# Eight gate rows, a block table and a tail: four batches' gates stored ahead, the dispatch reordered, the last two blocks in one branch

## The chip, the cores and the metric

The kernel runs on one core of a Trainium2 chip. The metric is the device time of one execution in microseconds. The core has five engines that run at once and meet at semaphores: TensorE (PE: matmuls and transposes into PSUM banks), VectorE (DVE), ScalarE (ACT), GpSimd (POOL) and SyncE (SP, which here only issues DMAs). PEld is the weight load of TensorE, which overlaps its matmuls.

## The reference, cut to what matters

```
u = stack([mean, max, std]) of each batch and channel, of the normalised x      # 8 batches, 512 channels
g = sigmoid(BN(sum((u - median(u)) ** 3 * cfc_w)))                              # one gate per batch and channel
x = x + ln_c(x) * g
t = tokens(x)                                                                   # 2048 tokens of 512
xn = ln_t(t)
e = argmax(xn @ router_w.T); w = sigmoid(max logit)                             # one of 8 experts
out = t + w * glu_e(xn) + glu_shared(xn)     # glu(x) = (silu(x @ wg) * (x @ wu)) @ wd, all 512x512
```

## The kernel before, in words

The host only lays the arrays out, tokens by channels. There are 16 tiles of 128 tokens (two to a batch) and, behind them, blocks of 128 tokens that are sorted by expert. Each engine has its own program, written out by hand in the order in which it runs; nothing is scheduled, so the order of the code is the order of the engine, and an instruction waits for the semaphores named ahead of it.

Stage 1 measures batches and channels. Stage 2 finds the median of each batch by a search of seven steps. On TensorE `keep_warm` puts matmuls into it whose results nobody reads. At its end ScalarE turns `z` into `gates` with Sigmoid and then loads the table of Silu with the small `warm` activation (L571). Meanwhile GpSimd makes the low parts of weight set 0 (L397), and `w_raw` holds the raw weights of a set, one third each for GATE, UP and DOWN.

Stage 3 takes the 16 tiles. For a tile, ScalarE normalises it (`norm_a`), VectorE multiplies it by the batch's gates and adds (`gate_tile`, L760 to L773), and normalises it again (`norm_tile`). The gates of a batch must be spread over all 128 tokens: `spread_gate(b)` on TensorE transposes four broadcast columns of `gates` into the bank `mb`, and `gate_tile` reads the bank. There is one such bank, so a batch's gates are spread only when the tiles of the batch before have used theirs (`gate_used`); `GATES_AFTER` says after which iteration n this happens. The tile is transposed (`prepare`, bank `tx`), split into a high and a low part (`x_hi` on ScalarE, `x_lo` on VectorE), multiplied by the shared expert's gate and up matrices (`gate_product`, `up_product`, bank `GU`, 12 matmuls each), gated (`silu_gate`, `gated`), transposed again (`transpose_h`, bank `th`), split again (`h_hi`, `h_lo`), multiplied by the down matrix (`down_product`, bank `yb`) and added (`add_shared`). `route` makes the router's logits, in `th` too.

Stage 4, the dispatch, runs among the last five tiles of the shared expert. `choose` picks the experts, `rank` on TensorE counts, for each token, the tokens ahead of it with the same expert, and, in 16 matmuls of their own (`COUNTS`, L1205), each expert's tokens. On VectorE `slots_of_tokens`, `place` and `fields` make matrices from that, `fill_slots` on TensorE (L1213) multiplies them, and `slot_tables`, `block_experts` and `block_table` make the indices and a table of blocks.

Stage 5 runs the blocks, 20 of them with these inputs. `groups` loops over 24 places. In the first 12 places `step` runs without a question; in the others each engine compares `needed` with the place. `step(b)` makes the gate and up products of block b + 1, transposes the hidden tile of block b and the input of block b + 2, and makes the down product of block b. `last(b)` has only the transpose and the down product. GpSimd gathers inputs (`gather_x`, `gather_z`) and scatters results (`scatter`).

The time of matmuls and transposes is best read from the start of one group to the start of the next.

Of the kernel before, what the change touches and what calls it, by code (L numbers as in the profile page):

```python
# [34 lines left out]
SPLIT_AFTER = (4, 5, 7)  # L35
GATES_AFTER = {0: 2, 2: 3, 3: 4, 5: 5, 6: 6, 8: 7}
# [7 lines left out]
def program(nc, B, x_tok, conv_par, router, weights, xn_d, z_d, out):  # L44
# [12 lines left out]
    with ExitStack() as ctx:  # L57
# [63 lines left out]
        slotinfo = sb("slotinfo", [P, 3, NB])  # L121
# [49 lines left out]
        z_ready = sem("z_ready")  # L171
        g_ready = sem("g_ready")
# [49 lines left out]

        def tally(i):

            return (yb, mb)[i % 2][:, i:i + 1]
# [43 lines left out]
        def groups(eng, step, last):  # L269


            needed = needed_blocks(eng)
            with eng.Fori(0, SURE // RING) as j:
                for u in range(RING):
                    step(j * RING + u, u, j, 0)
            with eng.Fori(0, (NB - SURE) // RING) as j:
                for u in range(RING):
                    b = j * RING + (SURE + u)
                    with eng.If(needed > b + 1):
                        step(b, u, j, SURE // RING)  # L280
                    with eng.If(needed == b + 1):
                        last(b, u, j, SURE // RING)
# [3 lines left out]
        def _(sp):  # L286
# [11 lines left out]
            for k in range(3):  # L298
                sp.wait_ge(wlo, k + 1)
                load_w(1, k)  # L300
# [26 lines left out]
        def _(pool):  # L327
# [124 lines left out]
            for b in range(NB):  # L452
# [25 lines left out]
        def _(act):  # L478
# [91 lines left out]
            act.activation(gates[:, :, :], z[:, :, :], ACT.Sigmoid, scale=-1.0).then_inc(g_ready, 1)  # L570
            act.activation(warm[:, 1:2], eps[:, 0:1], ACT.Silu).then_inc(warmed, 1)  # L571
# [45 lines left out]
            def last(b, u, j, base):  # L617
                h_hi(b + NT, u % 2)

            act.wait_ge(tables, 1)  # L620
            next_set(table_entries(act, 0, range(DUE_GU_COL, FIRST_COL + 1)))
            groups(act, step, last)
# [3 lines left out]
        def _(dve):  # L626
# [133 lines left out]
            def gate_tile(t, u, batch):  # L760
# [3 lines left out]
                dve.wait_ge(gates_spread, batch + 1)  # L764
                dve.tensor_tensor(buf, buf, mb[:, :], ALU.mult).then_inc(gate_used, 1)
# [159 lines left out]
            def slot_tables():  # L925
# [3 lines left out]
                tok, row, wgt = (slotinfo[:, i, :] for i in range(3))  # L929
# [54 lines left out]
            def add_routed(n, b, u, count):  # L984
                dve.wait_ge(y_done, n + 1)
                dve.wait_ge(zg_in[u], count)
                dve.scalar_tensor_tensor(out=zg[:, u, :], in0=yb[:, :], scalar=slotinfo[:, 2, ds(b, 1)], in1=zg[:, u, :],  # L987
                                         op0=ALU.mult, op1=ALU.add).then_inc(y_used, 1)
# [50 lines left out]
            groups(dve, step, last)  # L1039
# [3 lines left out]
        def _(pe):  # L1043
            pe.wait_ge(consts, N_CONSTS)

            def keep_warm(n):

                for _ in range(n):
                    pe.matmul(th[:, :], ones_bf[:, :], ones_bf[:, 0:1].to_broadcast([P, C]), start=True, stop=True)  # L1049
# [50 lines left out]
            def spread_gate(b):  # L1100

                if b == 0:
                    pe.wait_ge(g_ready, 1)
                else:
                    pe.wait_ge(gate_used, 2 * b)
                for k in range(KC):
                    last = pe.transpose(mb[:, k * P:(k + 1) * P], gates[:, b, k:k + 1].to_broadcast([P, P]), ident[:, :])  # L1107
# [16 lines left out]
            def product(dst, left, q, k):  # L1124

                i = 0
                for kc in range(KC):
                    for lp, wp in ((HI, HI), (HI, LO), (LO, HI)):
                        last = pe.matmul(dst, left[:, lp, kc, :], wset(q, k, wp, kc), start=(i == 0), stop=(i == 3 * KC - 1))  # L1129
                        i += 1  # L1130
                return last
# [11 lines left out]
            def down_product(n, parity, q, before):  # L1143
# [3 lines left out]
                product(yb[:, :], hT[:, parity], q, DOWN).then_inc(y_done, 1)  # L1147

            def route(t, slot):

                pe.wait_ge(xlo, t + 1)
                if not (isinstance(t, int) and t == 0):
# [13 lines left out]
            keep_warm(8)  # L1166
            spread_gate(1)
            keep_warm(2)
# [26 lines left out]
            def rank():  # L1195
# [61 lines left out]
            def last(b, u, j, base):  # L1257
# [5 lines left out]
            groups(pe, step, last)  # L1263
# [36 lines left out]
```

## Time and profile before

| what | value |
|---|---|
| median of 3 runs | 431.53 us (430.38 to 432.97) |
| the profiled execution | 430.49 us |
| its span, first to last instruction | 428.7 us |
| TensorE's mean granted clock in it | 0.965 of full speed |
| busy: PE, DVE, ACT, POOL | 384.1, 259.6, 158.2, 135.8 us |

Busy time is the sum of an engine's instructions. The profiled execution is 1.04 us below the median, and 1.8 us of it lie outside the span.

### The profile page before, as it was taken

To read this page: it belongs to the slowest core of one execution; us is meant where nothing else is said; L and a number is where in the kernel's file an instruction comes from. 1 tells how busy PE (TensorE), PEld (TensorE's weight loads), DVE (VectorE), ACT (ScalarE), POOL (GpSimd) and SP (SyncE) were. 2 spreads that over 40 slices of the span, in tenths; PEclk is the share of its full clock that TensorE was granted. 3 is DMA by queue.
4 is the path that set the end of the run, shared out by engine and by line. 5 is a ranking of instruction groups with operands and counts; after the bars stand their busy time and mean duration, and the time that the engine had idled before them with its cause. 6 is when DMAs were issued, how large, how long until landed. Compare 5 with 4: busy or idle time off the path is not lost.

```text
span 428.7 us, 6732 instructions
## 1 busy us (share of the span) xinstructions
PE 384.1 (90%) x1942; PEld 313.2 (73%) x1943; DVE 259.6 (61%) x494; ACT 158.2 (37%) x262; POOL 135.8 (32%) x188
## 2 busy tenths in 40 slices
PE   1455576999999999999989999999999999999993
PEld 1343134888888888888878888888888888888882
DVE  5995868455575795754686557636556653776322
ACT  4787861212223423221112335434144624354110
POOL 5676832000010010003112034633426442446201
PEclk9757988999999999999999999999999999999998
DMA  8900341011121342311004086765636764742300
GB/s 275 407 7 2 124 170 49 26 49 50 49 75 50 130 145 93 126 72 50 26 25 122 26 317 201 253 232 203 216 86 249 271 256 144 253 173 91 94 24 29
DMA packets 15865, 56.18 MB, mean 131 GB/s; under 512 B 2591, under 2 KB 2591, under 8 KB 12384
## 3 DMA queue, kind: packets, MB, share of 16 engines
q1 hardware_dynamic: 10960, 40.93, 26.8%
q0 software_dynamic: 4880, 14.95, 9.6%
q8 instruction: 13, 0.21, 0.2%
q14 instruction: 12, 0.10, 0.1%
HBM read 43.28 MB, written 13.63 MB: 133 GB/s over the span
## 4 chain that ended last, share of the span: by engine, by line
PE 80%; DVE 10%; issue 3%; ACT 3%; POOL 2%; DMA 1%; DVEq 0%; POOLq 0%; ACTq 0%
PE GU L1129 45%; PE yb L1129 22%; PE tx L1114 4%; PE th L1121 3%; PE th L1156 3%; DVE search_junk L709 1%; DVE bn_parts L664 1%; ACT tiles L492 1%; POOL tok_rstd L375 1%; DMA x_sb<-x_tok 1%; PE mb L1107 1%; PE th L1049 1%; DVE scratch L922 1%; ACT scratch L503 1%; DVE bn_parts L669 1%
## 5 line engine op out<-in xcount | busy, mean ns | idle before, releaser
L1129 PE MATMUL GU<-w_parts,xT 128*128 (+1 forms) x864 | 214.6, 398 | 0.0
L1129 PEld LDWEIGHTS GU<-w_parts,xT 128*128 128x128 f32 x864 | 159.4, 189 | 31.8
L1129 PE MATMUL yb<-w_parts,hT 128*128 (+1 forms) x432 | 105.4, 393 | 1.9 <-DVE hT L791 1.9
L563 ACT ACTIVATE hT<-th 128x512 fp32r<-128x512 f32 x36 | 21.5, 598 | 195.1 <-PE th L1121 195.1
L1129 PEld LDWEIGHTS yb<-w_parts,hT 128*128 128x128 f32 x432 | 80.1, 188 | 18.2 <-issue 2.1
L430 POOL DMA_INDIRECT out<-x_sb,scatidx x20 | 37.3, 1864 | 93.7 <-DVE x_sb L987 93.7
L812 DVE TENSOR_TENSOR w_parts<-w_raw,w_parts 128x2048 f32 (+1 forms) x24 | 54.9, 2288 | 6.7 <-issue 6.4
L797 DVE TENSOR_TENSOR hidden<-hidden,GU 128x512 f32<-128x512 f32 x36 | 24.8, 688 | 42.9 <-PE GU L1129 42.8
L480 ACT ACTIVATE w_parts<-w_raw 128x2048 f32 (+1 forms) x24 | 45.2, 1910 | 3.8 <-issue 3.7
L404 POOL TENSOR_TENSOR x_rstd<-x_mv,eps 128x1 f32<-128x1 f32 x16 | 3.2, 203 | 120.5 <-DVE x_mv L773 120.5
L791 DVE TENSOR_TENSOR hT<-th,hT 128x512 fp32r<-128x512 f32 x36 | 24.8, 688 | 23.1 <-ACT hT L563 23.0
L553 ACT ACTIVATE xT<-tx 128x512 fp32r<-128x512 f32 x37 | 22.0, 596 | 41.1 <-PE tx L1114 41.1
L987 DVE SCALAR_TENSOR_TENSOR x_sb<-yb,slotinfo,x_sb 128x512 f32<-128x512 f32 x20 | 15.0, 749 | 31.9 <-PE yb L1129 29.2
L1061 PE MATMUL GU<-ident,tiles 128*128 128x128 f32 x64 | 14.6, 406 | 21.3 <-ACT tiles L492 21.3
L1061 PEld LDWEIGHTS GU<-ident,tiles 128*128 128x128 f32 x64 | 12.0, 214 | 23.3 <-issue 16.0
L421 POOL DMA_INDIRECT tiles<-xn_d,tokidx x21 | 20.2, 961 | 24.3 <-DVE slotinfo L939 18.2
L425 POOL DMA_INDIRECT x_sb<-z_d,tokidx x20 | 19.4, 971 | 25.9 <-DMA z_d<-x_sb 20.1
L782 DVE TENSOR_TENSOR xT<-tx,xT 128x512 fp32r<-128x512 f32 x37 | 25.3, 683 | 3.5 <-ACT xT L553 3.4
L1114 PE MATMUL tx<-ident,tiles 128*128 128x128 f32 x148 | 22.7, 277 | 2.7 <-DVE xT L782 1.5
L802 DVE TENSOR_TENSOR x_sb<-x_sb,yb 128x512 f32<-128x512 f32 x16 | 11.0, 686 | 19.5 <-PE yb L1129 19.4
L558 ACT ACTIVATE hidden<-GU 128x512 f32<-128x512 f32 x36 | 21.7, 602 | 3.0 <-PE GU L1129 3.0
L1114 PEld LDWEIGHTS tx<-ident,tiles 128*128 128x128 f32 x148 | 17.9, 142 | 5.3 <-DVE tiles L778 3.4
(194 smaller groups left out, 352.2 us busy)
## 6 DMA issues: line engine op xcount, KB each, us to landing
w_raw<-weights SPq DMA_DIRECT2D x27, 1024.0 KB, 5.2
x_sb<-x_tok SPq DMA_DIRECT2D x8, 512.0 KB, 8.0
xn_d<-tiles SPq DMA_DIRECT2D x16, 256.0 KB, 2.0
z_d<-x_sb SPq DMA_DIRECT2D x16, 256.0 KB, 2.0
tiles<-xn_d,tokidx POOLq DMA_INDIRECT x21, 4.5
x_sb<-z_d,tokidx POOLq DMA_INDIRECT x20, 5.5
out<-x_sb,scatidx POOLq DMA_INDIRECT x20, 6.9
conv<-conv_par SPq DMA_DIRECT2D x1, 10.0 KB, 10.7
```

The costliest lines, as they stand in the source:

```text
L430: pool.indirect_dma_start(out[:, :], rows(scatidx, b), zg[:, b % RING, :], None, bounds_check=T - 1, oob_is_err=False).then_inc(o_out[b % ...
L480: act.activation(hi, raw, ACT.Copy).then_inc(whi, 1)
L553: act.activation(xT[:, slot, HI, :, :], tx[:, :].rearrange("p (k t) -> p k t", k=KC), ACT.Copy).then_inc(xhi, 1)
L558: act.activation(hidden[:, parity, :], gu(parity, GATE), ACT.Silu).then_inc(silu, 1)
L563: act.activation(hT[:, parity, HI, :, :], th[:, :].rearrange("p (k t) -> p k t", k=KC), ACT.Copy).then_inc(hhi, 1)
L782: dve.tensor_tensor(xT[:, slot, LO, :, :], tx[:, :].rearrange("p (k t) -> p k t", k=KC), xT[:, slot, HI, :, :].bitcast(F32), ALU.subtract) ...
L791: dve.tensor_tensor(hT[:, parity, LO, :, :], th[:, :].rearrange("p (k t) -> p k t", k=KC), hT[:, parity, HI, :, :].bitcast(F32), ALU.subtr ...
L797: dve.tensor_tensor(hidden[:, parity, :], hidden[:, parity, :], gu(parity, UP), ALU.mult).then_inc(hid_ready, 1)
L812: dve.tensor_tensor(lo, w_raw[:, k, :, :], hi.bitcast(F32), ALU.subtract).then_inc(wlo, 1)
L1061: last = pe.transpose(aT[:, k, h * P:(h + 1) * P], tiles[:, t % RING, k * P:(k + 1) * P], ident[:, :])
L1114: last = pe.transpose(tx[:, k * P:(k + 1) * P], src[:, k * P:(k + 1) * P], ident[:, :])
L1129: last = pe.matmul(dst, left[:, lp, kc, :], wset(q, k, wp, kc), start=(i == 0), stop=(i == 3 * KC - 1))
```

## The change

There are four parts.

1. Gates. `spread_gate` of batches 2 to 5 moves ahead of the first tile. It goes into bank `th`, ScalarE copies each one into the DOWN third of `w_raw` (free once set 0 is split), and `gate_tile` reads it there. `gates_stored` passes between them. Batches 0, 1, 6 and 7 still use `mb`. SyncE loads the DOWN third of set 1 later, ahead of `store_z(6)`, when tile 11 has used its gates; ScalarE and VectorE split it one iteration later (`SPLIT_AFTER`).
2. Counts. The 16 matmuls of `COUNTS` go; the matmuls of the ranks are made one tile wider and one more is added.
3. Order on VectorE in the dispatch.
4. `last_two` in place of `last`: the last two blocks in one branch. The transpose of the last hidden tile stands in the middle of the down product ahead of it, the last down product goes into `mb`, and the input of a block behind the last is neither gathered nor transposed.

```
-SPLIT_AFTER = (4, 5, 7)
-GATES_AFTER = {0: 2, 2: 3, 3: 4, 5: 5, 6: 6, 8: 7}
+SPLIT_AFTER = (4, 5, 8)
+GATES_AFTER = {6: 6, 8: 7}
+STORED_GATES = range(2, 6)
...
+        def gate_rows(batch):
+
+            return w_raw[:, DOWN, batch - STORED_GATES.start, :] if batch in STORED_GATES else mb[:, :]
...
-                    with eng.If(needed > b + 1):
+                    with eng.If(needed > b + 2):
                         step(b, u, j, SURE // RING)
-                    with eng.If(needed == b + 1):
-                        last(b, u, j, SURE // RING)
+                    with eng.If(needed == b + 2):
+                        last_two(b, u, j, SURE // RING)
...
-            for k in range(3):
+            for k in (GATE, UP):
                 sp.wait_ge(wlo, k + 1)
                 load_w(1, k)
...
+                if STORED_GATES.stop * 2 - 1 in (PREPARED[n] if n < len(PREPARED) else ()):
+                    sp.wait_ge(wlo, 3)
+                    sp.wait_ge(gate_used, STORED_GATES.stop * 2)
+                    load_w(1, DOWN)
...
-                    with pool.If(needed > c):
+                    with pool.If(needed > c + 1):
                         fetch_x(c + 1)
...
             act.activation(gates[:, :, :], z[:, :, :], ACT.Sigmoid, scale=-1.0).then_inc(g_ready, 1)
+            act.wait_ge(wlo, 3)
+            for b in STORED_GATES:
+                act.wait_ge(gates_spread, b)
+                act.activation(gate_rows(b), th[:, :], ACT.Copy).then_inc(gates_stored, 1)
             act.activation(warm[:, 1:2], eps[:, 0:1], ACT.Silu).then_inc(warmed, 1)
...
-                dve.wait_ge(gates_spread, batch + 1)
-                dve.tensor_tensor(buf, buf, mb[:, :], ALU.mult).then_inc(gate_used, 1)
+                if batch in STORED_GATES:
+                    dve.wait_ge(gates_stored, batch - STORED_GATES.start + 1)
+                else:
+                    dve.wait_ge(gates_spread, batch + 1 if batch > 1 else 1 + batch * (len(STORED_GATES) + 1))
+                dve.tensor_tensor(buf, buf, gate_rows(batch), ALU.mult).then_inc(gate_used, 1)
...
             gated(n + 1, 0)
+            slots_of_tokens()
             add_shared(n)
-            slots_of_tokens()
+            place()
             h_lo(n + 1, 0)
-            place()
+            fields()
             gated(n + 2, 1)
-            fields()
             add_shared(n + 1)
...
-            def last(b, u, j, base):
+            def last_two(b, u, j, base):
                 h_lo(b + NT, u % 2)
+                gated(b + (NT + 1), 1 - u % 2)
+                h_lo(b + (NT + 1), 1 - u % 2)
                 add_routed(b + NT, b, u, j * 16 + 16 * (base + 1))
+                add_routed(b + (NT + 1), b + 1, (u + 1) % RING, j * 16 + 16 * (base + 1 + (u + 1) // RING), mb)
...
             spread_gate(0)
-            keep_warm(8)
+            for b in STORED_GATES:
+                spread_gate(b)
+                keep_warm(1, yb)
             spread_gate(1)
-            keep_warm(2)
+            keep_warm(2, yb)
...
-                for i in range(NT - 1):
-                    pe.matmul(mb[:, (i + 1) * E:NT * E].rearrange("p (t e) -> p t e", e=E), ones_bf[:, :],
-                              oh[:, i * E:(i + 1) * E].unsqueeze(1).to_broadcast([P, NT - 1 - i, E]),
-                              start=False, stop=(i == NT - 2))
+                pe.matmul(mb[:, COUNTS], ones_bf[:, :], oh[:, 0:E], start=False, stop=False)
                 for i in range(NT):
-                    last = pe.matmul(mb[:, COUNTS], ones_bf[:, :], oh[:, i * E:(i + 1) * E], start=(i == 0), stop=(i == NT - 1))
+                    after = NT - (i == 0) - i
+                    last = pe.matmul(mb[:, (i + 1) * E:(i + 1 + after) * E].rearrange("p (t e) -> p t e", e=E), ones_bf[:, :],
...
-            def last(b, u, j, base):
-                at, = table_entries(pe, b, range(SET_COL, SET_COL + 1))
-                transpose_h(b + NT, u % 2)
-                down_product(b + NT, u % 2, at % 2, at * 3)
+            def last_two(b, u, j, base):
+                n = b + NT
+                at, after = table_entries(pe, b, range(SET_COL, SET2_COL + 1))
+                gate_product(n + 1, 1 - u % 2, 1 - u % 2, after % 2, after * 3)
+                transpose_h(n, u % 2)
+                up_product(n + 1, 1 - u % 2, 1 - u % 2, after % 2, after * 3)
+                down_product(n, u % 2, at % 2, at * 3, lambda: transpose_h(n + 1, 1 - u % 2))
+                pe.wait_ge(wlo, after * 3 + 3)
+                pe.wait_ge(hlo, n + 2)
+                product(mb[:, :], hT[:, 1 - u % 2], after % 2, DOWN).then_inc(y_done, 1)
```

Three places show what the engines issue in which order. The first is TensorE at the passage from stage 2 to stage 3. Before:

```order
L1049 MATMUL th<-ones_bf 128x512 x9
L1107 MATMUL mb<-ident,gates 128x128 x4
L1049 MATMUL th<-ones_bf 128x512 x8
L1107 MATMUL mb<-ident,gates 128x128 x4
L1049 MATMUL th<-ones_bf 128x512 x2
L1114 MATMUL tx<-ident,tiles 128x128 x8
L1129 MATMUL GU<-w_parts,xT 128x512 x12
```

The same place of the changed kernel, from the second spread on (the first two rows stand there four times):

```order
L1134 MATMUL th<-ident,gates 128x128 x4
L1071 MATMUL yb<-ones_bf 128x512
...
L1134 MATMUL mb<-ident,gates 128x128 x4
L1071 MATMUL yb<-ones_bf 128x512 x2
L1141 MATMUL tx<-ident,tiles 128x128 x8
L1156 MATMUL GU<-w_parts,xT 128x512 x12
```

Eight matmuls of `keep_warm` became four spreads with one such matmul behind each, and each of these spreads but the first waits for ScalarE's copy of the one before it. The second place is VectorE in the dispatch, from the last instruction of `slots_of_tokens` to `add_shared(n + 1)`. Before:

```order
L900 CAST tiles<-tiles 128x32
L791 TENSOR_TENSOR hT<-th,hT 128x512
L904 TENSOR_TENSOR scratch<-iota_f,tiles 128x2048
L906 TENSOR_TENSOR tiles<-iota_f,tiles 128x384
L797 TENSOR_TENSOR hidden<-hidden,GU 128x512
...
L922 TENSOR_TENSOR scratch<-tiles 128x16x24 x6
L802 TENSOR_TENSOR x_sb<-x_sb,yb 128x512
```

After:

```order
L919 CAST tiles<-tiles 128x32
L821 TENSOR_TENSOR x_sb<-x_sb,yb 128x512
L923 TENSOR_TENSOR scratch<-iota_f,tiles 128x2048
L925 TENSOR_TENSOR tiles<-iota_f,tiles 128x384
L810 TENSOR_TENSOR hT<-th,hT 128x512
...
L941 TENSOR_TENSOR scratch<-tiles 128x16x24 x6
L816 TENSOR_TENSOR hidden<-hidden,GU 128x512
L821 TENSOR_TENSOR x_sb<-x_sb,yb 128x512
```

`slots_of_tokens` now stands ahead of the first addition of `yb`, `place` ahead of the split of `th`, and `fields` ahead of the product with `GU`. The third place is TensorE in the branch of the changed kernel for the last two blocks, around the middle of the first down product (the rows marked ISA set up a register):

```order
L1156 MATMUL yb<-w_parts,hT 128x512 x2
L1148 MATMUL th<-ident,hidden 128x128 x4
L1156 ISA
L1156 MATMUL yb<-w_parts,hT 128x512
...
L1156 MATMUL yb<-w_parts,hT 128x512 x2
L1297 REGISTER_ALU
L1156 ISA
L1156 MATMUL mb<-w_parts,hT 128x512
```

Before, the four transposes of `hidden` stood behind the whole down product, in a branch of their own.

## Rows read from the trace of the kernel before

**Rows 1.** Page, part 1: busy time, share of the span and instructions of each engine

```profile
PE 384.1 (90%) x1942; PEld 313.2 (73%) x1943; DVE 259.6 (61%) x494; ACT 158.2 (37%) x262; POOL 135.8 (32%) x188
```

**Rows 2.** Timeline of PE inside the loop of tiles: start us, us, engine, line

```profile
91.34 0.60 PE L1107 MATMUL mb<-ident,gates 128*128 128x128 f32 x4
91.69 1.04 PE L1156 MATMUL th<-router_parts,xT 128*128 128x16 f32 x8
```

**Rows 3.** Timeline of PE, end of stage 2 to the first products

```profile
63.90 2.12 PE L1049 MATMUL th<-ones_bf 128*128 128x512 bf16 x8
...
69.61 0.66 PE L1114 MATMUL tx<-ident,tiles 128*128 128x128 f32 x4 [1.16 <-DVE tiles L778]
71.78 1.08 PE L1114 MATMUL tx<-ident,tiles 128*128 128x128 f32 x4 [1.50 <-DVE xT L782]
72.51 3.96 PE L1129 MATMUL GU<-w_parts,xT 128*128 128x512 f32 x12
```

**Rows 4.** Timeline of ACT in the same stretch

```profile
62.41 1.28 ACT L571 ACT_TABLE_LOAD   x1
63.70 0.20 ACT L571 ACTIVATE warm<-eps 128x1 f32<-128x1 f32 x1
70.31 0.60 ACT L553 ACTIVATE xT<-tx 128x512 fp32r<-128x512 f32 x1 [6.41 <-PE tx L1114]
```

**Rows 5.** Windows of PE: stretch, its length, busy, granted clock, DMA share, GB/s

```profile
43.00:55.50 12.50, 6.67 (x33) 1.00 0.46 168
...
67.70:71.20 3.50, 1.42 (x9) 0.99 0.20 75
71.20:74.60 3.40, 2.82 (x9) 0.50 0.20 77
```

**Rows 6.** Timeline of PE in the dispatch

```profile
204.66 0.54 PE L1205 MATMUL mb<-tiles,ones_bf 128*128 128x8 bf16 x16
205.06 2.97 PE L1129 MATMUL yb<-w_parts,hT 128*128 128x512 f32 x12
...
216.50 2.88 PE L1129 MATMUL GU<-w_parts,xT 128*128 128x512 f32 x12
220.66 1.17 PE L1213 MATMUL mb<-scratch 128*128 128x144 bf16 x16 [1.27 <-DVE scratch L922]
```

**Rows 7.** Timeline of DVE in the dispatch

```profile
204.36 0.69 DVE L797 TENSOR_TENSOR hidden<-hidden,GU 128x512 f32<-128x512 f32 x1 [1.52 <-PE GU L1129]
...
208.68 0.28 DVE L888 TENSOR_TENSOR tiles<-tile_start,mb 128x128 f32<-128x128 f32 x1
...
211.96 0.69 DVE L791 TENSOR_TENSOR hT<-th,hT 128x512 fp32r<-128x512 f32 x1
...
215.35 0.69 DVE L797 TENSOR_TENSOR hidden<-hidden,GU 128x512 f32<-128x512 f32 x1
...
217.70 2.90 DVE L922 TENSOR_TENSOR scratch<-tiles 128x384 bf16<-128x384 bf16 x6
```

**Rows 8.** Timeline of PE over the last three blocks

```profile
406.32 2.88 PE L1129 MATMUL yb<-w_parts,hT 128*128 x12
409.05 2.89 PE L1129 MATMUL GU<-w_parts,xT 128*128 x12
411.77 0.60 PE L1121 MATMUL th<-ident,hidden 128*128 128x128 f32 x4
...
412.56 3.01 PE L1129 MATMUL GU<-w_parts,xT 128*128 x12
415.41 2.89 PE L1129 MATMUL yb<-w_parts,hT 128*128 x12
418.14 0.60 PE L1121 MATMUL th<-ident,hidden 128*128 128x128 f32 x4
420.62 3.03 PE L1129 MATMUL yb<-w_parts,hT 128*128 x12 [1.89 <-DVE hT L791]
```

**Rows 9.** Timeline of DVE, the last hidden tile

```profile
415.68 0.69 DVE L797 TENSOR_TENSOR hidden<-hidden,GU 128x512 f32<-128x512 f32 x1 [1.35 <-PE GU L1129]
```

More of the change, by code:

```diff
@@ L171, in program @@
         z_ready = sem("z_ready")
+        gates_stored = sem("gates_stored")
         g_ready = sem("g_ready")
@@ L267, in needed_blocks, with groups @@
             return table_entries(eng, 0, range(TOTAL_COL, TOTAL_COL + 1))[0]
-        def groups(eng, step, last):
+        def groups(eng, step, last_two):
             needed = needed_blocks(eng)
@@ L615, in step @@
                 next_set(table_entries(act, b + 1, range(DUE_GU_COL, FIRST_COL + 1)))
-            def last(b, u, j, base):
+            def last_two(b, u, j, base):
                 h_hi(b + NT, u % 2)
+                silu_gate(b + (NT + 1), 1 - u % 2)
+                h_hi(b + (NT + 1), 1 - u % 2)
             act.wait_ge(tables, 1)
             next_set(table_entries(act, 0, range(DUE_GU_COL, FIRST_COL + 1)))
-            groups(act, step, last)
+            groups(act, step, last_two)
         @block.vector
@@ L928, in slot_tables @@
                 S = mb[:, SLOTS].rearrange("p (f b) -> p f b", f=FIELDS)
-                tok, row, wgt = (slotinfo[:, i, :] for i in range(3))
+                tok, row, wgt = (slotinfo[:, i, 0:NB] for i in range(3))
                 own(dve.tensor_copy(tok, S[:, 0, :]))
@@ L982, in block_table, with add_routed @@
                 dve.engine_nop().then_inc(tables, 1)
-            def add_routed(n, b, u, count):
+            def add_routed(n, b, u, count, bank=yb):
                 dve.wait_ge(y_done, n + 1)
                 dve.wait_ge(zg_in[u], count)
-                dve.scalar_tensor_tensor(out=zg[:, u, :], in0=yb[:, :], scalar=slotinfo[:, 2, ds(b, 1)], in1=zg[:, u, :],
+                dve.scalar_tensor_tensor(out=zg[:, u, :], in0=bank[:, :], scalar=slotinfo[:, 2, ds(b, 1)], in1=zg[:, u, :],
                                          op0=ALU.mult, op1=ALU.add).then_inc(y_used, 1)
@@ L1038, in _ @@
                 lo_of(DOWN, at)
-            groups(dve, step, last)
+            groups(dve, step, last_two)
         @block.tensor
@@ L1044, in _, with keep_warm @@
             pe.wait_ge(consts, N_CONSTS)
-            def keep_warm(n):
+            def keep_warm(n, bank=th):
                 for _ in range(n):
-                    pe.matmul(th[:, :], ones_bf[:, :], ones_bf[:, 0:1].to_broadcast([P, C]), start=True, stop=True)
+                    pe.matmul(bank[:, :], ones_bf[:, :], ones_bf[:, 0:1].to_broadcast([P, C]), start=True, stop=True)
             for b in range(B):
@@ L1103, in spread_gate @@
                     pe.wait_ge(g_ready, 1)
+                elif b in STORED_GATES:
+                    pe.wait_ge(gates_stored, b - STORED_GATES.start)
+                elif b == STORED_GATES.stop:
+                    pe.wait_ge(gate_used, 4)
                 else:
                     pe.wait_ge(gate_used, 2 * b)
+                bank = th if b in STORED_GATES else mb
                 for k in range(KC):
-                    last = pe.transpose(mb[:, k * P:(k + 1) * P], gates[:, b, k:k + 1].to_broadcast([P, P]), ident[:, :])
+                    last = pe.transpose(bank[:, k * P:(k + 1) * P], gates[:, b, k:k + 1].to_broadcast([P, P]), ident[:, :])
                 last.then_inc(gates_spread, 1)
@@ L1122, in transpose_h, with product @@
                 last.then_inc(th_done, 1)
-            def product(dst, left, q, k):
+            def product(dst, left, q, k, amid=None):
                 i = 0
@@ L1130, in product @@
                         i += 1
+                    if kc == 1 and amid:
+                        amid()
                 return last
@@ L1141, in up_product, with down_product @@
                 product(gu(parity, UP), xT[:, slot], q, UP).then_inc(u_done, 1)
-            def down_product(n, parity, q, before):
+            def down_product(n, parity, q, before, amid=None):
                 pe.wait_ge(wlo, before + 3)
                 pe.wait_ge(hlo, n + 1)
-                product(yb[:, :], hT[:, parity], q, DOWN).then_inc(y_done, 1)
+                product(yb[:, :], hT[:, parity], q, DOWN, amid).then_inc(y_done, 1)
             def route(t, slot):
                 pe.wait_ge(xlo, t + 1)
-                if not (isinstance(t, int) and t == 0):
+                if t == 0:
+                    pe.wait_ge(gates_stored, len(STORED_GATES))
+                else:
                     pe.wait_ge(logits_used, t)
```

8 lines of the change are left out of this document (5 added, 3 removed).

## The prediction, as it was made before the changed kernel ran

> **What bounds the kernel now.** I read the page's busy times first, then the chain that ended last, then the timelines of TensorE and of the engine that releases it at the places which the diff touches. TensorE is busy 90% of the span [rows 1]; between the first product and the end nearly every group on it starts where the one before ends. So what is taken out of its queue there is gained whole. It waits in three places that this change touches: before the first product [rows 3], at `fill_slots` in the dispatch [rows 6], and before the last down product [rows 8]. The sum is made against the profiled execution, 430.49 us, which lies 1.04 us below the median of 431.53.
>
> **Gates in the loop.** A spread takes 0.35 us of TensorE's queue, 91.34 to 91.69 [rows 2]. Four of six leave the loop, each of them between groups that run back to back: 4 x 0.36 = 1.4 us less. The readers lose nothing: `gate_tile` multiplies from SBUF instead of a bank, for which I take no price (bounds: 0, or 0.1 us for each of 8 tiles on VectorE, which in this stage waits for TensorE). The copies' room is the DOWN third of `w_raw`. Its load for set 1 moves behind tile 11, in SyncE's queue ahead of `store_z(6)` and of all later stores; one issue there delays stores that nobody needs before the dispatch ends. The split of it moves from iteration 8 to 9 of 11; its user is the first routed down product, many products later. Both at nothing.
>
> **Gates before the first tile.** This is the part that costs. Four rounds of spread, copy, spread run one behind the other, since `th` is one bank. From the start of four transposes to the start of ScalarE's conversion it takes 0.70 us (69.61 to 70.31), an ACT conversion of 128x512 takes 0.60 [rows 3, 4], and a transpose that waited for VectorE started about 0.15 after it: 1.45 a round. The first begins where the keep-warm matmuls begin now, 63.90 [rows 3], and, at the lower clock, takes about 0.25 more. The last copy ends at 63.90 + 0.25 + 4 x 1.45 - 0.15 = 69.8. Behind it in ScalarE's queue stand the load of Silu's table, 1.28, and `warm`, some 0.1 before the next can start [rows 4], so `x_hi(0)` starts at 71.2, not at 70.31. `x_lo(0)` and the transposes of tile 1 follow it, so those start at about 72.67 instead of 71.78 [rows 3]: 0.9 us later. What was hidden between 62.4 and 70.3 (the table load) is no longer.
> What follows depends on the clock. Now it is at the lower level (1.2 GHz, 0.50 granted) from 71.2 to 74.6, after a stretch in which TensorE was busy 1.42 of 3.50 us; in the search it was busy 6.67 of 12.5 and stayed at 2.4 GHz [rows 5]. The first product takes 3.96 us there against 2.88 later [rows 3, 6]. In the new order TensorE has, between 64 and 70.5, five spreads, six keep-warm matmuls and the transposes of tile 0 at even distances, some 0.9 us of busy time in a round of 1.45 by the same count (0.60 for a spread, 0.27 for one matmul), more than in the search. I hold it likelier than not that it stays at 2.4 GHz. Then tile 1 takes 0.36, the product starts at 73.0 and the next group at 75.9, instead of 72.51 + 3.80 = 76.3: 0.45 gained in spite of the later start. If the lower level comes where it came before, half of the 0.9 is lost, 0.4; if it only moves along, all 0.9.
> A rule speaks against this part. The Trainium skill, "ScalarE: Activation LUTs", section What ACT_TABLE_LOAD costs, puts a switch of table at 1283 ns and a drain of 1380 ns more. The trace has 62.41 to 63.70, 1.29 us, with no drain before the next activation [rows 4]. With the page's figure as an estimate the first conversion would come 1.38 later still and the sum below would be smaller by that.
>
> **Counts with ranks.** The 16 matmuls of the counts take 204.66 to 205.06, 0.40 us, 25 ns each [rows 6]. Two are added, 0.05, and the others are 8 columns wider, about 0.03 in all: 0.32 less. Waits on them end earlier too.
>
> **Dispatch order.** `fill_slots` starts at 220.66; the product ahead of it starts at 216.50 and takes 2.72 to the next start when nothing waits [rows 6, 8]: 1.44 us of stall, which ends with the last of the field products of VectorE, 217.70 + 2.90 = 220.60 [rows 7]. Before, `add_shared(n)` stood first and waited for the down product that starts at 205.06, so `slots_of_tokens` began at 208.68, though its input was there. Now it begins when `gated(n+1)` ends, 204.36 + 0.69 = 205.05 [rows 7]. From its start to the end of the fields it has the same work as before, two 128x512 operations included: 220.60 - 208.68 = 11.92. So the fields are ready at 217.0, where TensorE comes at 218.9 (0.32 earlier than 219.22 by the counts): no stall, and 1.9 us in hand. Who is late next? `h_lo(n+1)` starts 205.05 + (211.96 - 208.68) + (215.35 - 211.96) = 211.7 and ends by 212.4; its product comes at 213.5: 1 us in hand less the 0.3 of a semaphore. `gated(n+2)` ends at 217.7, and its transpose now stands behind `fill_slots`, 219.9. All times here move along with the 1.4 of the gates. 1.44 less.
>
> **The last two blocks.** The transposes of a block behind the last go: `th` and `tx` together take 411.77 to 412.56, 0.79, and one alone 0.36 [rows 8, 2], so 0.43 less. The last hidden tile is transposed after 6 of the 12 matmuls, 1.36 us earlier. It is ready by then: the product on VectorE ends 415.68 + 0.69 - 0.43 = 415.9 [rows 9], the six matmuls end at 415.41 - 0.43 + 1.36 = 416.3. From this transpose to the last down product it takes 418.14 to 420.62, 2.48 (conversion, split, semaphores) [rows 8], so that starts at 418.8 instead of 420.62: 1.8 less. 0.25 more is possible, since VectorE's addition and branches stood ahead of that split before. The rest of the down product ahead ends at 418.1, so 0.5 to 0.7 of stall stays. The addition, the scatter and the end follow as before. The last down product can't be late for the bank, since `mb` has been idle since the dispatch.
>
> **Sum.** 1.4 + 0.3 + 1.44 + 1.8 = 5.0 us, and 0.45 from the first product at the full clock: 5.45. From the median that gives 426.1, from the profiled execution 425.0.
>
> **Rivals.**
> 1. The clock falls all the same, or the chain of copies is slower than 1.45 a round: the start costs 0.4 to 0.9 instead of bringing 0.45. Gain 4.1 to 4.6, time 426.9 to 427.4. For it speaks that the transposes of tile 1 now stand behind 2.2 us without work on TensorE (70.5 to 72.7), against 1.50 before [rows 3]. Chance 0.30.
> 2. One of the two larger terms isn't there: the dispatch waits for something else (`h_lo` has only 0.7 us in hand), or the last split waits behind the addition. Gain 3.6 to 4.0, time 427.5 to 428. Against it: each queue was followed above. Chance 0.12.
> 3. Slower than before: the branch for the last two blocks. In each of the places 12 to 17 TensorE's sequencer must jump over it, and its body has grown from 16 to 52 matmuls and transposes. Now such a jump costs 0.01: the product behind it starts 2.73 after the one before, where one without a jump takes 2.72 [rows 8]. The upper bound is the longest wait that rows of TensorE show here, 1.89. Six of those would be 11.3 and the time 437.4; from 0.91 us a jump on, the change loses, and from 1.27 on by over 0.5%. Chance 0.03. The Trainium skill, "Runtime: NRT & Kernel Launch", section Instruction fetch mechanics, says that a taken branch to a page outside the current two forces a fetch before execution goes on; by that rule the longer jump is more exposed than the old one, whose rows show no such stop.
> 4. No change beyond what can be measured, if several terms shrink or the start costs over 3 us (say rounds of 2.2). Chance 0.06.
>
> **How the numbers follow.** The forecast, with its own range 425.0 to 426.8, has 0.49. The point is 426.1. Downwards the range goes by the 0.25 of the last split and by the lower base of the profiled execution: 424.6. Upwards it takes in rivals 1 and 2: 428.2. A measurement of this kernel can tell about 0.5%, 2.2 us, from no change, 429.4. Faster: 0.49 + 0.30 + 0.12 = 0.91, less 0.02 for a rival 2 with both terms gone: 0.89. Same 0.07, slower 0.04.
>
> **What would show it.** Right: no idle time before the `fill_slots` matmuls; the down product of the first iteration followed at once by `route`; the last down product, into `mb`, starting about 0.5 to 0.7 after the one before it ends; the first x conversion at about 71.2 with the table load directly before it, and full clock behind it. Wrong: a copy round over 1.6 us, a drain behind the table load, a clock of 0.5 over the first product, a wait on `h_lo` in the dispatch, or gaps on TensorE at the jumps between blocks 12 and 18.

## The result, and the profile after

The changed kernel takes 425.10 us in median (423.48 to 425.89, 6 runs), the kernel before beside it 431.65 us (430.38 to 433.08, 6 runs). The ratio is 0.9861, with a 95% interval of 0.9833 to 0.9890, so it is 1.4% faster. Word for word again, at another time, it gave 424.49 us (423.50 to 425.99, 6 runs) against 430.46, ratio 0.9856 (0.9824 to 0.9888). The prediction was 426.1 in a range from 424.6 to 428.2. One execution of the kernel before, among the 17 beside `q_keepwarm_before`, `q_noamid`, `q_warmfirst` and `q_gu`, took 1842 us and is left out of the ratios and counts below.

The page of the changed kernel, its head and the row of the granted clock in 40 slices:

```profile
span 423.6 us, 6668 instructions
...
PE 385.3 (91%) x1920; PEld 313.0 (74%) x1921; DVE 258.9 (61%) x493; ACT 160.1 (38%) x265; POOL 135.2 (32%) x187
...
PEclk9999799999999999999999999999999999999999
```

The same row of the kernel before:

```profile
PEclk9757988999999999999999999999999999999998
```

Each digit is the clock that TensorE was granted in a slice, in tenths of full speed. The two rows differ already in slices 2 to 5, ahead of all that the change touches.

The profiled execution took 425.56 us, and its span is 5.1 us shorter than before. This is the timeline of TensorE at the passage to the first product, to be read against [rows 3] (start, us, engine and line):

```profile
60.80 0.32 PE L1108 MATMUL tx<-ident,search 128*128 128x128 f32 x1 [1.14 <-DVE search L758]
...
64.68 0.94 PE L1134 MATMUL th<-ident,gates 128*128 128x128 f32 x4
...
66.37 0.65 PE L1134 MATMUL th<-ident,gates 128*128 128x128 f32 x4 [0.53 <-ACT w_raw L584]
...
69.05 0.65 PE L1134 MATMUL th<-ident,gates 128*128 128x128 f32 x4 [0.47 <-ACT w_raw L584]
...
70.62 0.60 PE L1141 MATMUL tx<-ident,tiles 128*128 128x128 f32 x4
73.20 0.63 PE L1141 MATMUL tx<-ident,tiles 128*128 128x128 f32 x4 [1.98 <-DVE xT L801]
73.58 2.99 PE L1156 MATMUL GU<-w_parts,xT 128*128 128x512 f32 x12
76.41 0.95 PE L1187 MATMUL th<-router_parts,xT 128*128 128x16 f32 x8
```

ScalarE's timeline there, to be read against [rows 4]:

```profile
69.73 0.60 ACT L584 ACTIVATE w_raw<-th 128x512 f32<-128x512 f32 x1 [0.74 <-PE th L1134]
70.35 1.28 ACT L585 ACT_TABLE_LOAD   x1
71.64 0.20 ACT L585 ACTIVATE warm<-eps 128x1 f32<-128x1 f32 x1
71.75 0.58 ACT L563 ACTIVATE xT<-tx 128x512 fp32r<-128x512 f32 x1
```

The four spreads stand 1.34 us apart from the second on. The table load lies directly ahead of `warm` and the first conversion. The first product, granted the full clock, takes 2.83 us to the next start. For the dispatch and the end, these rows of TensorE are to be read against [rows 6] and [rows 8]:

```profile
202.81 0.23 PE L1232 MATMUL mb<-tiles,upper 128*128 128x128 bf16 x1
202.88 0.17 PE L1233 MATMUL mb<-tiles,ones_bf 128*128 128x8 bf16 x1
202.91 0.70 PE L1236 MATMUL mb<-tiles,ones_bf 128*128 128x120 bf16 x16
203.46 2.97 PE L1156 MATMUL yb<-w_parts,hT 128*128 128x512 f32 x12
...
214.90 2.88 PE L1156 MATMUL GU<-w_parts,xT 128*128 128x512 f32 x12
217.62 1.17 PE L1246 MATMUL mb<-scratch 128*128 128x144 bf16 x16
...
403.45 2.88 PE L1156 MATMUL yb<-w_parts,hT 128*128 x12
406.17 2.89 PE L1156 MATMUL GU<-w_parts,xT 128*128 x12
408.89 0.60 PE L1148 MATMUL th<-ident,hidden 128*128 128x128 f32 x4
409.25 3.02 PE L1156 MATMUL GU<-w_parts,xT 128*128 x12
412.10 1.52 PE L1156 MATMUL yb<-w_parts,hT 128*128 x6
413.46 0.60 PE L1148 MATMUL th<-ident,hidden 128*128 128x128 f32 x4
413.82 1.64 PE L1156 MATMUL yb<-w_parts,hT 128*128 x6
415.67 2.99 PE L1156 MATMUL mb<-w_parts,hT 128*128 x12 [0.21 <-DVE hT L810]
```

The idle time before the `fill_slots` matmuls (217.62) is gone, and before the last down product 0.21 us are left of 1.89.

Cut at such starts, the two profiled executions differ as follows. The last median transpose is the last one of `search` into `tx`; the first route is the first group with the router's parts.

| stretch of TensorE | before | after | difference |
|---|---|---|---|
| start to last median transpose | 59.89 | 60.80 | +0.91 |
| to the first route | 16.42 | 15.61 | -0.81 |
| to the rank matmuls | 127.78 | 126.40 | -1.38 |
| the rank matmuls | 0.97 | 0.65 | -0.32 |
| to `fill_slots` | 15.60 | 14.16 | -1.44 |
| to the transposes of block 18 | 191.11 | 191.27 | +0.16 |
| to the last down product | 8.85 | 6.78 | -2.07 |
| to the end | 8.08 | 7.93 | -0.15 |

The first row is work that the change doesn't touch, and 0.87 of its 0.91 us stand in two rows, the kernel before first, then the changed one. They are the transposes of the statistics ahead of the search:

```profile
40.95 1.51 PE L1075 MATMUL GU<-ident,scratch 128*128 128x128 f32 x12 [2.46 <-DVE scratch L697]
41.02 2.38 PE L1097 MATMUL GU<-ident,scratch 128*128 128x128 f32 x12 [1.99 <-DVE scratch L713]
```

So the two profiled executions had the lower clock at different places of stages 1 and 2, and the 5.1 us are not all the change's. The +0.16 over the blocks isn't either: that stretch takes 191.11 to 191.40 us in the fourteen profiles, with no order by kernel.

### The profile page after: what moved, and what is told of

Same layout as the page of the kernel before. It is cut to its first block, busy times and chain, and to the rows that moved or that the text cites. A ratio compares the mean times of both kernels' runs of the same rounds, so it can differ in the third digit from the quotient of the medians.

```text
span 423.6 us, 6668 instructions
## 1 busy us (share of the span) xinstructions
PE 385.3 (91%) x1920; PEld 313.0 (74%) x1921; DVE 258.9 (61%) x493; ACT 160.1 (38%) x265; POOL 135.2 (32%) x187
## 4 chain that ended last, share of the span: by engine, by line
PE 84%; DVE 6%; ACT 3%; issue 3%; POOL 2%; DMA 1%; DVEq 0%; POOLq 0%; ACTq 0%
PE GU L1156 47%; PE yb L1156 23%; PE th L1148 4%; PE tx L1141 4%; PE th L1187 3%; DVE search_junk L725 2%; DVE bn_parts L680 1%; ACT tiles L502 1%; POOL tok_rstd L385 1%; DMA x_sb<-x_tok 1%; PE mb L1156 1%; ACT scratch L513 1%; PE th L1071 1%; DVE bn_parts L685 1%; PE th L1134 1%
## 5 line engine op out<-in xcount | busy, mean ns | idle before, releaser
L1156 PE MATMUL yb<-w_parts,hT 128*128 (+1 forms) x420 | 102.7, 393 | 0.0
L1156 PEld LDWEIGHTS yb<-w_parts,hT 128*128 128x128 f32 x420 | 77.8, 188 | 15.7
L1083 PE MATMUL GU<-ident,tiles 128*128 128x128 f32 x64 | 15.3, 423 | 20.7 <-ACT tiles L502 20.7
L431 POOL DMA_INDIRECT tiles<-xn_d,tokidx x20 | 19.3, 964 | 22.3 <-DVE slotinfo L958 16.5
L1141 PE MATMUL tx<-ident,tiles 128*128 128x128 f32 x144 | 21.6, 273 | 2.0 <-DVE xT L801 2.0
L1148 PE MATMUL th<-ident,hidden 128*128 128x128 f32 x144 | 21.5, 272 | 0.0
L1148 PEld LDWEIGHTS th<-ident,hidden 128*128 128x128 f32 x144 | 17.8, 140 | 4.6
```

What stands on the lines that cost most here:

```text
L1083: last = pe.transpose(aT[:, k, h * P:(h + 1) * P], tiles[:, t % RING, k * P:(k + 1) * P], ident[:, :])
L1141: last = pe.transpose(tx[:, k * P:(k + 1) * P], src[:, k * P:(k + 1) * P], ident[:, :])
L1148: last = pe.transpose(th[:, k * P:(k + 1) * P], hidden[:, parity, k * P:(k + 1) * P], ident[:, :])
```

## The experiments

### The four parts alone, each on the kernel before

```
p_gates:    SPLIT_AFTER, GATES_AFTER, STORED_GATES, gate_rows, the late load_w(1, DOWN), the four copies, the new waits
p_last_two: groups, last_two on PE, ACT and DVE, fetch_x(c + 1) if needed > c + 1
p_dispatch: the order of slots_of_tokens, place and fields
p_counts:   rank() with the counts in it
```

> The kernel before with the gates part alone. My theory: four spreads of 0.35 us leave TensorE's queue in the loop, so from the first route to the rank matmuls it is 1.4 us shorter (127.8 before, 126.4); the start costs 0.5 us more up to the transposes of tile 1, and, if the clock stays at 2.4 GHz over the first product, gives back 1.3: 2.2 us less than before in all, ratio 0.995. Rival (the changed kernel's fall in median, 6.5 us against the 5.0 to 5.45 of my sum, lies in a chance of runs): only 1.4 less. Second rival: the gates part gives all of the excess, 3 us or more less, ratio 0.993.

> The kernel before with the branch for the last two blocks alone. My theory: from the transposes of block 18 to the start of the last down product 6.8 us instead of 8.85, so 2.1 less, ratio 0.995, and no gap on TensorE at the jumps between blocks 12 and 18 (9.06 us a block as before). Rival, longer jumps cost fetches: blocks 12 to 17 take more than 9.1 us each and the gain is smaller or gone.

> The kernel before with the new order of VectorE in the dispatch alone. My theory: the idle time of 1.27 us before the fill_slots matmuls is 0, their start comes 4.16 us after the product ahead of them before and 2.72 now, 1.44 less, ratio 0.9967. Rival: the wait moves to h_lo or to the slot tables and less than 0.5 is left.

> The kernel before with the counts merged into the rank matmuls alone. My theory: from the first rank matmul to the down product 0.65 us instead of 0.97, but nothing of the whole: the wait of fill_slots on VectorE, which started its slots only after an addition of the down product, shifts too, so 0.3 less at most. Rival: 0, since the stall ahead of fill_slots grows by what the counts give. Neither can be told by the time (under 0.1%), only by the idle time before fill_slots: 1.27 as before by the first, 1.6 by the second.

Measured over 12 runs each against 35 of before on the same chip (431.30 us in median), and cut in the profile as in the table above:

| kernel | median us | ratio (95% interval) | last median transpose to first route | to ranks | ranks | to `fill_slots` | block 18 to last product | last product to end |
|---|---|---|---|---|---|---|---|---|
| p_gates | 430.01 | 0.9974 (0.9948 to 0.9999) | 15.6 | 126.39 | 0.97 | 15.60 | 8.85 | 9.68 |
| p_last_two | 428.35 | 0.9943 (0.9919 to 0.9966) | 15.3 | 127.80 | 0.97 | 15.60 | 6.78 | 8.00 |
| p_dispatch | 431.51 | 1.0014 (0.9988 to 1.0039) | 15.3 | 127.80 | 0.98 | 14.16 | 8.82 | 9.65 |
| p_counts | 431.19 | 1.0012 (0.9986 to 1.0039) | 15.3 | 127.81 | 0.65 | 15.60 | 8.82 | 8.08 |

Each part does in its own stretch about what the sum said: 1.4, 2.07, 1.44 and 0.32 us. But the medians don't follow. They are 1.3, 2.95, -0.2 and 0.1 us below the kernel before, 4.1 in all, and the changed kernel gained 6.5. By the ratios, `p_gates` and `p_last_two` are faster clear of noise; the other two can't be told from the kernel before. `p_dispatch` was to be 1.44 us faster and gained nothing at all, although its stall is gone. Its last column says where it went. This is the timeline of TensorE at the end of `p_dispatch`:

```profile
415.56 0.60 PE L1121 MATMUL th<-ident,hidden 128*128 128x128 f32 x4
...
418.05 4.61 PE L1129 MATMUL yb<-w_parts,hT 128*128 x12 [1.89 <-DVE hT L791]
```

The last down product takes 4.61 us where it took 3.03 before [rows 8]. The windows of TensorE there (stretch, length, busy, granted clock, DMA share, GB/s) say why:

```profile
416.00:418.00 2.00, 0.16 (x2) 1.00 0.00 0
418.00:420.00 2.00, 1.95 (x6) 0.66 0.36 135
420.00:422.70 2.70, 2.66 (x8) 0.62 0.00 0
```

Behind the idle 1.89 us most of its matmuls ran at the lower clock, 1.2 GHz. The same happened in the profile of `p_gates` (4.60). `p_last_two` and the changed kernel, which have 0.21 us idle there, show about 3.0. In `p_dispatch` this eats the gain in all twelve executions, not only in the profiled one: they took 429.3 to 433.1 us as the kernel before did, group by group, each group with a mean granted clock that is 0.003 to 0.005 lower (0.961 for 0.966 at 429.4 us, 0.986 for 0.990 at 430.7, 0.974 for 0.978 at 433.0). The windows above lack 1.7 us of full clock, which is 0.004 of the span. The branch for the last two blocks takes the gap away.

The other finding is in the column of the first route. The kernel before and three of these four run the same program up to there. They need 15.3 in three profiles and 16.42 in that of the kernel before, whose first product ran at 0.50 [rows 5]. In `p_dispatch` the same two groups start as follows:

```profile
72.33 2.98 PE L1129 MATMUL GU<-w_parts,xT 128*128 128x512 f32 x12
75.15 0.95 PE L1156 MATMUL th<-router_parts,xT 128*128 128x16 f32 x8
```

That is 2.82 us for the product, where [rows 3] have 3.80. So the profile on which the prediction stands held a fall of the clock worth 1.15 us that others don't have.

The jumps in `p_last_two` and in the changed kernel cost nothing: behind a jump the product starts 2.72 us after the one before (403.45 to 406.17), as in [rows 8], and the blocks take 9.05 to 9.09 us each. One block of each took 9.2; `p_counts`, which has the old branch, has one of 9.3.

### The clock before the first product and before the last

```
q_keepwarm_before (on before)
             spread_gate(1)
-            keep_warm(2)
+            keep_warm(6)
             prepare(0)
+            keep_warm(5)
             prepare(1)
r_warm_last (on before, in last)
                 transpose_h(b + NT, u % 2)
+                for _ in range(8):
+                    pe.matmul(mb[:, :], ones_bf[:, :], ones_bf[:, 0:1].to_broadcast([P, C]), start=True, stop=True)
                 down_product(b + NT, u % 2, at % 2, at * 3)
r_warm_both: both edits
```

> The kernel before with nine more keep-warm matmuls between the spread of batch 1 and the transposes of tile 1, and nothing else. Tests what the clock at the first product is worth. My theory: the granted clock stays 1.00 from 64.3 us on, the first product takes 2.9 instead of 3.96, and the kernel is 1.3 us faster than before (428.5 with the profiled execution's base). Rival: the fall of the clock there comes in some executions only, then the medians differ by 0.5 or less; or the matmuls delay the transposes by up to 0.3.

> The kernel before with eight keep-warm matmuls, into mb, between the transposes of the last hidden tile and the last down product, where TensorE is idle for 1.9 us; nothing else. In two of five profiled executions of kernels with that idle time the last down product took 4.6 us instead of 3.0, at a lower clock. My theory: the clock falls there in a part of the executions of the kernel before, and filling the gap takes that away: profile with 3.0, median 0.5 to 0.8 us below before, highest times 1 us lower. Rival: the 4.6 belongs to the two kernels where it was seen, and the median stays.

> The kernel before with keep-warm matmuls both before the first product (as in the run with nine of them) and before the last down product; nothing else. My theory: both falls of the clock are gone, 428.8 us in median, 2.5 below before; the changed kernel is then only 3.7 below this one instead of 6.5 below before, and some 2.5 of its gain were clock that its order keeps up by the way. Rival: clock falls are noise that both kernels share, then this one lies less than 1 us below before.

`q_keepwarm_before` took 429.40 us against 431.58, ratio 0.9966 (0.9948 to 0.9984), or 1.5 us by the ratio where 1.3 was expected. The windows of TensorE in its profile (stretch, length, busy, granted clock, DMA share, GB/s), to be read against [rows 5]:

```profile
67.70:71.20 3.50, 3.21 (x18) 1.00 0.20 75
71.20:74.60 3.40, 2.98 (x16) 1.00 0.20 77
```

Nine matmuls whose results nobody reads, put into idle time, make the kernel 0.3% faster. Of its 12 executions one took over 431 us, of the kernel before beside it 9 of 16.

`r_warm_last` took 431.77 against 430.46, ratio 1.0028 (1.0005 to 1.0052): no gain, rather a small loss, with 9 of 12 executions over 431 where the kernel before beside it had 7 of 23. The last down product took 3.01 in its profile, but no execution of the kernel before is known in which it took more. So the theory falls for the kernel before, and the rival stands. In these profiles the gap of 1.89 us did harm only in kernels that come to it at another time, as `p_gates` and `p_dispatch` did.

`r_warm_both` took 429.85 us, ratio 0.9982 (0.9963 to 1.0001), and none of 12 executions took over 430.85. Expected were 2.5 us below the kernel before, and it came out 0.6, which is what the rival said and not clear of noise. The kernel before beside it had only 4 of 23 executions of the long kind that is told below.

Most executions fall on few levels, which the time and the mean granted clock tell apart together:

| kernel | levels, us (mean granted clock) |
|---|---|
| before (35 runs) | 429.3 (0.966 to 0.97) x8, 430.4 (0.965) x2, 430.6 (0.985 to 0.99) x6, 431.5 (0.954 or 0.981 to 0.986) x10, 433.0 (0.978) x8, one at 430.9 |
| r_warm_last (12) | 429.4 (0.97) x2, 430.9 (0.99), 431.3 (0.981) x2, 431.9 (0.954) x4, 433.1 (0.978) x2, one at 432.2 |
| r_warm_both (12) | 428.3 (0.997), 429.5 (0.961 to 0.97) x5, 430.5 (0.985 to 0.987) x6 |
| after (12 in two sets) | 423.5 (0.999) x3, 424.5 (0.962 to 0.967) x4, 425.8 (0.984 to 0.991) x5 |

The profiles show what two of these levels are. Nine of them have a mean clock of 0.961 to 0.970. In these the clock is low from 15 or 16 to 37 or 40 us, at full speed again at the twelve transposes ahead of the search, which take 1.5 us, and the last median transpose comes at 59.8 to 59.9. The other five (0.987 to 0.990; the changed kernel both times, `q_noamid`, `r_warm_both`, `r_all`) have the full clock up to 40 us and the lower one at these transposes, which take 2.4 to 2.8 us, and the last median transpose comes at 60.7 to 61.2. So the level with the lower mean clock is the faster one, by 0.8 to 1.4 us, since its low stretch ends before these transposes. The profile of the kernel before (430.49 us, 0.965) is one of the nine, with the fall at the first product on top. It fits the small level at 430.4.

Compared level by level, `r_warm_both` and the changed kernel are 4.7 to 5.0 us apart, and the kernel before and the changed one 4.8 (429.3 to 424.5, 430.6 to 425.8). That is the work taken out. The rest of the gain is that the long executions of the kernel before go away. They are told by a mean clock up to 0.958 or from 0.974 to 0.980, bounds that were drawn after seeing the lists; in the kernel before they took 431.3 us and more. The kernel before has 15 of them in 35, 8 in 16 and 4 in 23, beside the three groups of kernels; `p_last_two`, `p_dispatch`, `p_counts` and `r_warm_last`, which leave the start as it was, have 21 in 48. The kernels that feed TensorE more between the search and the first product (`q_keepwarm_before`, `r_warm_both`, `p_gates`, the changed kernel and its four variants) have none in 70. How much that is in the median depends on the set of runs beside which one compares: 1.7 us of the 6.5 in the first, 1.2 of the 6.0 in the second.

### The end of the changed kernel

```
q_noamid (on after)
-                down_product(n, u % 2, at % 2, at * 3, lambda: transpose_h(n + 1, 1 - u % 2))
+                down_product(n, u % 2, at % 2, at * 3)
+                transpose_h(n + 1, 1 - u % 2)
```

> The changed kernel with the last hidden tile's transposes behind the whole down product again, in the same branch and bank. My theory: moving them to the middle bought 1.36 us of the 2.07 at the end; so from the transposes of block 18 to the last down product 8.0 to 8.2 us instead of 6.8, and the kernel is 1.2 us slower than the changed one. Rival: the branch alone (no table reads and jumps between the last two blocks) bought it, then 0.3 or less.

It took 426.60 us (6 runs), 1.5 above the first median of the changed kernel and 1.2 to 1.6 above it level by level (426.1 against 424.5, 427.0 against 425.8). The timeline of TensorE at its end:

```profile
409.07 0.60 PE L1148 MATMUL th<-ident,hidden 128*128 128x128 f32 x4
...
415.00 0.60 PE L1148 MATMUL th<-ident,hidden 128*128 128x128 f32 x4
417.20 3.03 PE L1156 MATMUL mb<-w_parts,hT 128*128 x12 [1.60 <-DVE hT L810]
```

From block 18 to the last product it takes 8.13 us instead of 6.78. The place in the middle of the product is worth 1.35, and the rival, that the branch alone bought the gain, falls. The rest of the 2.07 is 0.72: the transposes that went, 0.43, and some 0.3 that fit VectorE's split, which starts without the addition and the branches ahead of it. No run takes these two apart.

### The start of the changed kernel

```
q_warmfirst (on after)
+            act.activation(warm[:, 1:2], eps[:, 0:1], ACT.Silu).then_inc(warmed, 1)
             act.wait_ge(wlo, 3)
             for b in STORED_GATES:
                 act.wait_ge(gates_spread, b)
                 act.activation(gate_rows(b), th[:, :], ACT.Copy).then_inc(gates_stored, 1)
-            act.activation(warm[:, 1:2], eps[:, 0:1], ACT.Silu).then_inc(warmed, 1)
q_gu: also the four spreads into the four banks of GU, none waiting for a copy; keep_warm(7), (4), (3)
r_all: also batches 6 and 7 (by th and yb, kept in scratch); keep_warm(4), (4), (3)
```

> The changed kernel with the load of Silu's table moved ahead of the four copies, into ScalarE's idle time before the first one (2.43 us in the changed kernel). My theory: the load, 1.28 us, is hidden, the first x conversion is set by TensorE's queue, 0.7 after its transposes of tile 0 instead of 1.1, so 0.4 us less than the changed kernel. Rival: a table switch also drains or the copy needs another table, then two more loads and 1 us or more slower.

> The changed kernel with the four spreads in the four banks of GU, so that no spread waits for a copy, the table load first, and keep-warm matmuls (7, 4, 3) in the gaps. My theory: the first x conversion comes 10.4 us after the last median transpose, as in the kernel before (10.95 in the changed one), and the clock stays at 2.4 GHz: 0.5 us less than the changed kernel, about what the variant with the table load first gives. Rival: the copies hold ScalarE so long that the first conversion is late all the same: no gain.

> The changed kernel with the gates of six batches stored ahead (batches 6 and 7 in scratch), the spreads in four banks of GU, th and yb so that none waits for a copy, the table load before the copies, and 11 keep-warm matmuls in the gaps. My theory: two more spreads leave the loop, 0.7 us, and the first conversion is 0.35 earlier than in the changed kernel: 1.1 us less than it, 424.0. Rival: the longer row of spreads and copies makes the first conversion late by 0.5 or more and the gain is gone.

`q_warmfirst` took 424.25 us (5 runs), `q_gu` 424.25 (5 runs). Expected were 0.4 and 0.5 us less than the changed kernel, whose medians are 425.10 and 424.49, so the medians don't decide; the trace does. ScalarE's timeline of `q_warmfirst`:

```profile
62.26 1.28 ACT L581 ACT_TABLE_LOAD   x1
63.56 0.20 ACT L581 ACTIVATE warm<-eps 128x1 f32<-128x1 f32 x1
64.68 0.60 ACT L585 ACTIVATE w_raw<-th 128x512 f32<-128x512 f32 x1 [0.92 <-PE th L1134]
...
70.34 0.60 ACT L563 ACTIVATE xT<-tx 128x512 fp32r<-128x512 f32 x1 [1.06 <-PE tx L1141]
```

The load is hidden, and nothing had to be loaded again for the copies. The first conversion comes 10.6 us after the last median transpose in both variants, as in the kernel before where the clock did not fall, against 10.95 in the changed kernel. So the load was the whole lateness of 0.36, and freeing the spreads from the copies adds nothing to that. The rival of a drain or of further loads falls.

`r_all` took 424.28 us (422.45 to 424.74), ratio to before 0.9843 (0.9811 to 0.9874), against 424.49 and 0.9856 of the changed kernel on the same chip. The medians don't tell the two apart. Level by level it is 1.0 to 1.4 us faster (422.45, 423.31, 424.2 to 424.7 against 423.5, 424.3 to 424.7, 425.7 to 426.0), and in the profile its loop is 0.85 us shorter (125.55 against 126.40), for two spreads, and the first conversion 0.43 earlier. It is the fastest kernel here by its stages, on six runs.

## Why the prediction was right

**Gates in the loop**: 1.4 expected, 1.38 to 1.41 measured in `p_gates` and in the changed kernel. Nobody waited for the stored rows or for the late load.

**Gates before the first tile**: a round was to take 1.45 us and took 1.34, since the spread behind a copy starts 0.05 after it and not 0.15. The first conversion was to be 0.9 later. It was 0.53 later than in the profile before, 0.36 later than in other profiles of that program. No drain showed behind the table load: 70.35 to 71.64 with nothing between. Of these 1.29 us, 0.36 cost time by `q_warmfirst`; the rest ScalarE would have waited for TensorE's transposes anyway. The Trainium skill, "ScalarE: Activation LUTs", section What ACT_TABLE_LOAD costs, gives the load of 1283 ns, which the trace has, and a drain of 1380 ns, which it has not. The first product did run at the full clock, and that stretch came out 0.81 shorter where I had 0.45. But the term was wrongly read. It was set against a fall of the clock in one profiled execution, which only 2 of the 35 later ones resemble (430.4 us at 0.965); against four other profiles of the same start (`p_last_two`, `p_dispatch`, `p_counts`, `r_warm_last`) this part costs 0.35 and gains nothing. What it gains by the clock is seen only over many runs: the long executions are gone. That this comes with the spreads and matmuls between the search and the first product is shown by the counts above, none in 70 against 48 in 122. But the levels at 431.5 and 433.0 were never caught in a profile, so where the clock falls in them stays open.

**Counts and dispatch order**: 0.32 and 1.44 expected, 0.32 and 1.44 measured. The wait did not move on: in the changed kernel VectorE ends its fields 2.0 us before TensorE comes (215.6 against 217.62). `p_counts` shows that the counts alone keep their 0.32 in the stretch, since the stall ahead of `fill_slots` stays:

```profile
219.22 1.17 PE L1213 MATMUL mb<-scratch 128*128 128x144 bf16 x16 [1.28 <-DVE scratch L922]
```

In the time, 0.32 us can't be seen.

**The last two blocks**: 1.8 expected with 0.25 more possible, 2.07 measured. From the last transposes to the last product it took 2.21 us (413.46 to 415.67) where the sum kept the old 2.48, so the 0.25 is there, and the stall that was to stay at 0.5 to 0.7 is 0.21.

**Sum**: 5.0 without the clock. By levels the work taken out is 4.7 to 5.0 us, the start's 0.35 included. The time came 1.0 us below the forecast of 426.1, and the missing part is the size of the clock's share: 0.45 in the sum, 1.2 to 1.7 in the medians. So the four terms of work were right, and the term of the clock had the right sign by luck: it was priced from a rare execution, and what it gained came from other executions, of which the prediction knew nothing. Rival 1, a start that costs, was half right: it does cost, 0.35, but the first product kept the full clock. Rival 3, the longer jumps, was wrong: the trace shows 2.72 us over a jump. The Trainium skill, "Runtime: NRT & Kernel Launch", section Instruction fetch mechanics, has a taken branch to a page outside the current two wait for a fetch. No such wait shows here, and whether these jumps leave the two pages no run here shows.

## What to carry to other kernels

Ahead of a sum, find out whether the profile holds a fall of the clock that other executions don't have: compare a stretch that several kernels share, and look at the list of runs for levels. Compare executions of one level with each other; two profiles of different levels differ by 0.9 us before the change begins. An edit that takes time out early can lose it again at a later idle gap; so close the gaps on TensorE first, or fill them, and judge a small edit by its own stretch of the trace, since one part alone (the dispatch order here) can show no gain and still carry 1.4 us in the whole.
A function table is best loaded where its engine waits anyway; putting copies ahead of the load moved a part of it, 0.36 us of 1.29, from idle time onto the critical path.

## What the runs showed of the hardware

TensorE's clock fell behind an idle stretch as short as 1.89 us in some kernels and not in others, which differ in when they come there: the last down product took 4.61 us in `p_dispatch` (granted 0.66 and 0.62) and 4.60 in `p_gates`, but 3.03 in the kernel before and 3.00 in `p_counts`, all behind 1.89 us of idle time. Executions of one program lie on three or four main levels 0.9 to 1.5 us apart, not spread evenly between their lowest and highest time. A lower mean granted clock doesn't mean a slower execution: at 0.966 the kernel before took 429.3 us and at 0.990 it took 430.6, because the twelve transposes ahead of the search ran at full clock in executions of the first kind (1.5 us) and at half clock in those of the second (2.4 to 2.8).
